# Masked cross-attention: the mask of the third key tile by a minimum over the exponentials

## The reference

```python
scores = jnp.einsum('bhqd,bhkd->bhqk', Q, K) * scale          # 16 x 16 x 100 x 361
scores = jnp.where(attn_mask[:, None, :, :], -jnp.inf, scores)
A = jax.nn.softmax(scores, axis=-1)
out = jnp.einsum('bhqk,bhkd->bhqd', A, V)
out = out.transpose(0, 2, 1, 3).reshape(Bv, Tq, Dm)
return jnp.einsum('btd,od->bto', out, Wo) + bo
```

## Time and profile before

| | before |
|---|---|
| median of three runs | 2042.7 us (2034.51 to 2044.05) |
| the profiled execution | 2037.27 us, its span 2035.6 us |
| masked cross-attention: first and last use of the mask on PE | 1520.3 and 1762.0 us |
| PE, DVE, ACT, POOL busy in the whole span | 76%, 47%, 26%, 25% |

### The profile page before, as it was taken

One profiled execution on the slowest core, in us unless ns is written; L12 is line 12 of the kernel. 1 busy time (PEld: TensorE's weight loads), 2 busy tenths in 40 slices (PEclk: granted clock), 3 DMA queues, 4 the chain that ended last, 5 costly groups with the idle time before them and its releaser, 6 DMA issues. The chain is left out here.

```text
span 2035.6 us, 33676 instructions
## 1 busy us (share of the span) xinstructions
PE 1553.0 (76%) x11689; PEld 1200.6 (59%) x11689; DVE 959.3 (47%) x2639; ACT 528.5 (26%) x1081; POOL 502.0 (25%) x448
## 2 busy tenths in 40 slices
PE   4898974799978846999999155677549999636992
PEld 2555642577755525888888132455227877535992
DVE  4446435677755621222222286566547777450111
ACT  1444231244432101211121011222114344211330
POOL 1112010322213552222221670100032332222003
PEclk9999996799988877999999577797769999857996
DMA  6754563766622205666665355543256565127994
GB/s 245 193 165 146 154 180 110 159 149 143 145 57 57 57 9 168 198 200 199 195 187 162 89 163 166 111 100 81 87 135 134 127 136 126 47 84 264 346 345 140
DMA packets 302577, 303.34 MB, mean 149 GB/s; under 512 B 130910, under 2 KB 273630, under 8 KB 296878
## 3 DMA queue, kind: packets, MB, share of 16 engines
q1 hardware_dynamic: 272142, 263.32, 46.3%
q0 software_dynamic: 19328, 28.35, 5.1%
q10 hardware_dynamic: 11040, 10.82, 1.6%
HBM read 217.29 MB, written 85.03 MB: 149 GB/s over the span
## 5 line engine op out<-in xcount | busy, mean ns | idle before, releaser
L1458 ACT ACTIVATE attn_prob<-attn_ps_prob 121x400 f32<-121x400 f32 (+2 forms) x448 | 221.7, 503 | 418.1 <-PE attn_ps_prob L1357 414.3
L1316 PE MATMUL attn_ps_score<-attn_k,attn_q 96*100 96x361 bf16 (+1 forms) x768 | 152.1, 304 | 69.3 <-DMA attn_k<-k_stack 59.7
L1357 PEld LDWEIGHTS attn_ps_prob<-attn_q,attn_k 128*121 128x121 bf16 (+2 forms) x1792 | 162.1, 137 | 36.5 <-issue 8.1
L2179 DVE TENSOR_TENSOR experts_up<-experts_act_,experts_ps_up 128x250 f32<-128x250 f32 x128 | 53.2, 415 | 266.7 <-ACT experts_act_ L2140 266.7
L1357 PE MATMUL attn_ps_prob<-attn_q,attn_k 128*121 128x100 bf16 (+2 forms) x1792 | 169.1, 219 | 4.5 <-DVE attn_q L1506 3.0
L1487 DVE TENSOR_REDUCE attn_nmax<-attn_ps_score 100x2 f32<-100x722 f32 (+1 forms) x160 | 145.7, 921 | 38.7 <-PE attn_ps_score L1316 37.3
L1479 DVE CUSTOM_DVE_ANT_0 attn_masked_score<-attn_ps_score,attn_mask 100x361 bf16<-100x361 f32 x256 | 124.6, 531 | 55.0 <-PE attn_ps_score L1316 44.3
L1590 POOL TENSOR_TENSOR attn_q<-attn_shift,consts_sb 32x800 bf16<-32x800 bf16 x64 | 97.1, 1518 | 187.1 <-DVE attn_shift L1512 187.1
L2068 POOL DMA_INDIRECT experts_xe<-ln_rows,experts_now x64 | 77.6, 1212 | 257.8 <-DVE experts_now L2171 232.7
L2097 PE MATMUL experts_ps_up<-experts_xt,experts_wg 128*128 128x250 f32 x512 | 130.7, 378 | 0.8 <-DVE experts_xt L2168 0.8
L2097 PE MATMUL experts_ps_up<-experts_xt,experts_wu 128*128 128x250 f32 x512 | 129.9, 376 | 0.0
(11 more groups left out here) (283 smaller groups left out, 2640.1 us busy)
## 6 DMA issues: line engine op xcount, KB each, us to landing
experts_w<-in_w SPq DMA_DIRECT2D x40, 1024.0 KB, 5.5
attn_k<-k_stack SPq DMA_DIRECT2D x64, 541.5 KB
k_stack<-mixer_part SPq DMA_DIRECT2D x32, 541.5 KB, 5.4
experts_wg<-in_wg SPq DMA_DIRECT2D x32, 512.0 KB
experts_wu<-in_wu SPq DMA_DIRECT2D x32, 512.0 KB
experts_wd<-in_wd SPq DMA_DIRECT2D x32, 512.0 KB, 5.2
attn_q<-q_stack SPq DMA_DIRECT2D x96, 150.0 KB
k_stack<-mixer_part SPq DMA_DIRECT2D x32, 361.0 KB, 6.0
```

The lines of the kernel that those rows point to most:

```text
L1316: ins = nc.tensor.matmul(out, q_sb[s][0:SHIFT_ROW, h // HH, h % HH, :], k_sb[s][0:SHIFT_ROW, h // HH, h % HH, :], start=True, stop=True)
L1357: ins = nc.tensor.matmul(out[0:rows_, j * T:(j + 1) * T], k_sb[s][:, h // HH, h % HH, at:at + rows_], q_sb[s][:, h // HH, h % HH, :], star ...
L1458: nc.scalar.activation(prob[0:rows_, q4 % 2, t, :], ps_prob[k % 2][0:rows_, 0:GT], ACT.Exp, scale=DH ** -0.5).then_inc(a_prob[s], 1)
```

## The change

The mask of the third key tile no longer enters the score bank by a matmul. The exponentials of this tile are taken of the unmasked scores, and VectorE then sets the masked ones to zero by a minimum (`weigh`, L1547 of the changed kernel) with a table `upper`, which holds 0 where a key is masked and 3e38 elsewhere. The table is made once per batch element: TensorE transposes the third tile of the mask into PSUM (`turn_mask`, L1370), VectorE compares and scales it (L1539). The first two tiles keep their mask matmul. `weigh_values` now waits for the minimum (`v_weight`) before its third tile. `WEIGH_AT` puts the minima of quarters 0, 1 and 2 at the start of slots 4, 7 and 10 of VectorE's order, that of quarter 3 at the start of the next step.

```diff
--- before.py
+++ after.py
@@ -1162,6 +1162,7 @@
 
     at_unit = {-(-(u + 1) * (NPU - (NKT > 1)) // NU) - 1: u for u in range(NU)}
     shift_by_vector = layer == 1
+    WEIGH_AT = {4: 0, 7: 1, 10: 2}
     if NKT > 1:
         LAST_AV, SHIFT_B, ROWS, TURN, OUT, SHIFT_A = 1, 2, 3, 5, 7, 9
         av_at = {3 * g + 4: g for g in range(NQ - 1)}
@@ -1193,6 +1194,7 @@
         ones_set = sem("ones_set")
         g_order = sem("g_order")
         v_apart = sem("v_apart")
+        pe_upper, v_upper, v_weight = pair("pe_upper"), pair("v_upper"), pair("v_weight")
 
         q_sb = [sbuf(f"q{s}", [P, 2, HH, T], BF16) for s in range(2)]
         k_sb = [sbuf(f"k{s}", [P, 2, HH, NK], BF16) for s in range(2)]
@@ -1213,6 +1215,7 @@
         if masked:
             mask8 = [sbuf(f"mask8_{s}", [T, NK], U8) for s in range(2)]
             mask = [sbuf(f"mask{s}", [T, NK], BF16) for s in range(2)]
+            upper = [sbuf(f"upper{s}", [P, T]) for s in range(2)]
             masked_score = sbuf("masked_score", [T, HH, NK], BF16)
         ps_score = psum("ps_score", [P, 4, 512])
         ps_prob = [psum(f"ps_prob{k}", [P, 512]) for k in range(2)]
@@ -1349,16 +1352,23 @@
                     elif n_prev is not None:
                         pe.wait_ge(a_prob[1 - s], n_prev * NPU + k - 1)
                     out = ps_prob[k % 2]
-                    if masked:
+                    by_matmul = masked and t < NKT - 1
+                    if by_matmul:
                         nc.tensor.matmul(out[0:rows_, 0:GT], mask[s][:, at:at + rows_], prog.c("tile_diag")[0:T, :],
                                          start=True, stop=False)
                     for j in range(G):
                         h = q4 * G + j
                         ins = nc.tensor.matmul(out[0:rows_, j * T:(j + 1) * T],
                                                k_sb[s][:, h // HH, h % HH, at:at + rows_],
-                                               q_sb[s][:, h // HH, h % HH, :], start=not masked,
-                                               stop=not masked or j == G - 1)
+                                               q_sb[s][:, h // HH, h % HH, :], start=not by_matmul,
+                                               stop=not by_matmul or j == G - 1)
                     ins.then_inc(pe_prob[s], 1)
+
+                def turn_mask(s, n):
+                    at, rows_ = KEYS[NKT - 1]
+                    pe.wait_ge(g_mask[s], n)
+                    nc.tensor.transpose(ps_misc[:].bitcast(BF16)[0:rows_, 0:T], mask[s][:, at:at + rows_],
+                                        ident_b[0:T, 0:T]).then_inc(pe_upper[s], 1)
 
                 def weigh_values(s, n, q4, n_prev):
                     if q4 == 0:
@@ -1366,7 +1376,10 @@
                         if n_prev is not None:
                             pe.wait_ge(a_acc[1 - s], n_prev)
                     for t, (_, rows_) in enumerate(KEYS):
-                        pe.wait_ge(a_prob[s], n * NPU + (q4 * NKT + t + 1 - NPU))
+                        if masked and t == NKT - 1:
+                            pe.wait_ge(v_weight[s], n * NQ + (q4 + 1 - NQ))
+                        else:
+                            pe.wait_ge(a_prob[s], n * NPU + (q4 * NKT + t + 1 - NPU))
                         for j in range(G):
                             ins = nc.tensor.matmul(ps_acc[32 * j:32 * j + 32, q4 * T:(q4 + 1) * T],
                                                    val[s][0:rows_, t, q4 * G + j, :],
@@ -1399,6 +1412,9 @@
                     for u in range(NU):
                         score_unit(s, n, u, n_cur)
                     shift_rows(s, n, 0)
+                    if masked:
+                        pe.wait_ge(v_shift[0][s], n)
+                        turn_mask(s, n)
                     values(s, n)
 
                 def step(s, n, n_prev, n_next):
@@ -1410,6 +1426,8 @@
                             weigh_values(s, n, av_at[k], n_prev)
                         if k == SHIFT_B:
                             pe.wait_ge(v_shift[0][s], n)
+                            if masked:
+                                pe.wait_ge(v_upper[s], n)
                             shift_rows(s, n, 1)
                         if n_prev is not None:
                             if k == ROWS:
@@ -1430,6 +1448,9 @@
                                     pe.wait_ge(v_shift[1][s], n)
                                 shift_rows(1 - s, n_next, 0)
                     if n_next is not None:
+                        if masked:
+                            pe.wait_ge(v_shift[0][1 - s], n_next)
+                            turn_mask(1 - s, n_next)
                         values(1 - s, n_next)
 
                 def tail(s, n):
@@ -1512,6 +1533,20 @@
                     nc.vector.tensor_copy(shift[h][SHIFT_ROW:P, :], ps_misc[:].bitcast(BF16)[SHIFT_ROW:P, 0:T]
                                           ).then_inc(v_shift[h][s], 1)
 
+                def turn_mask(s, n):
+                    rows_ = KEYS[NKT - 1][1]
+                    ve.wait_ge(pe_upper[s], n)
+                    nc.vector.tensor_scalar(upper[s][0:rows_], ps_misc[:].bitcast(BF16)[0:rows_, 0:T], 0.0, 3e38,
+                                            ALU.is_ge, ALU.mult).then_inc(v_upper[s], 1)
+
+                def weigh(s, n, q4):
+                    rows_ = KEYS[NKT - 1][1]
+                    ve.wait_ge(v_upper[s], n)
+                    ve.wait_ge(a_prob[s], n * NPU + ((q4 + 1) * NKT - NPU))
+                    here = prob[0:rows_, q4 % 2, NKT - 1, :].rearrange("p (g t) -> p g t", g=G)
+                    nc.vector.tensor_tensor(here, here, upper[s][0:rows_].unsqueeze(1).broadcast_to([rows_, G, T]),
+                                            ALU.min).then_inc(v_weight[s], 1)
+
                 def values(s, n):
                     for t, (_, rows_) in enumerate(KEYS):
                         ve.wait_ge(pe_val[s], n * NKT - (NKT - 1 - t))
@@ -1543,10 +1578,17 @@
                     for u in range(NU):
                         score_unit(s, n, u)
                     shift_rows(s, n, 0)
+                    if masked:
+                        turn_mask(s, n)
                     values(s, n)
 
                 def step(s, n, n_prev, n_next):
                     for k in range(NPU):
+                        if masked:
+                            if k == 0 and n_prev is not None:
+                                weigh(1 - s, n_prev, NQ - 1)
+                            if k in WEIGH_AT:
+                                weigh(s, n, WEIGH_AT[k])
                         if k == SHIFT_B:
                             shift_rows(s, n, 1)
                         if n_prev is not None:
@@ -1562,9 +1604,13 @@
                             if k == SHIFT_A:
                                 shift_rows(1 - s, n_next, 0)
                     if n_next is not None:
+                        if masked:
+                            turn_mask(1 - s, n_next)
                         values(1 - s, n_next)
 
                 def tail(s, n):
+                    if masked:
+                        weigh(s, n, NQ - 1)
                     to_rows(s, n)
                     turn(s, n)
                     project(s, n)
```

## The result

| | before | after |
|---|---|---|
| median of the runs | 2042.72 us (2034.51 to 2044.05, 4 runs) | 2123.89 us (2122.0 to 2125.4, 4 runs) |
| profiled execution, its span | 2037.27, 2035.6 | 2122.0, 2120.3 |
| mean granted clock | 0.875 | 0.861 |

A forecast was written before the change was run, and what follows sets the result against it. TensorE was taken to bound the masked stage. Its step was to grow from 15.56 to 19.9 us: +65 us over fifteen steps and 1.5 in the last, +67 on the 2042.7 median, giving 2110 us, range 2090 to 2142.

The forecast's parts named there:

- The walk: Masked cross-attention step followed in four legs between third-tile releases: period 19.9 us instead of 15.56, +4.36 us.
- guess of 0.08 us: Gap between a minimum's end and TensorE's start, guessed within 0 and 0.16; moves the sum by 5 us at most.
- near tie: Quarter 2 to quarter 3: TensorE's own work takes 3.81 us, just shorter than 3.93 us up to the minimum's release.
- hidden as said: VectorE's 16 tables, near 0.22 us each, cost nothing behind a 0.44 us wait for TensorE; uncovered, 3.5 us.
- The 10.9 us of removed matmuls: TensorE time freed by dropping the third tile's 64 mask matmuls at 0.17 us each, 0.68 us per step.
- Rival 1: Masked stage slows just as the walk says: 2110 us, own range 2098 to 2122; chance 0.60.
- rival 2: TensorE's clock falls in two to five masked-stage steps, adding 12 to 29 us: 2122 to 2139 us; chance 0.22.
- self-attention's busy share: Masked stage would fall to TensorE busy 15.0 of 19.9, the share of self-attention, which has a stretch at clock 0.59.
- Rival 3: GpSimd gets the ports first at quarter 2; a minimum waits up to 1.52 us, +23 us: 2133 us; chance 0.06.
- the lock: VectorE and GpSimd share SBUF ports exclusively; two-SBUF-input minima are concerned, but at quarter 2 it should cost nothing.
- Rival 4: Some stalls vanish as VectorE catches up; two of four legs at old length, +33: 2076 us; chance 0.07.
- Rival 5: TensorE finds the minima done; each step 0.53 us shorter, 8.5 us in all: 2034 us; chance 0.05.

The follow-up runs named there:

- e1_free: Changed kernel, but weighted sums do not wait for the minima, which read a tile of ones and write unread tiles; ratio 0.9988 to the kernel before.
- e6_late_sums: Changed kernel with TensorE's weighted sums moved to later slots, minima left where they stood; ratio 1.0008 to the kernel before.
- e7_both: Changed kernel with later weighted sums and earlier minima; ratio 0.9990 to the kernel before, steps 15.26 us.
- r_filler: Rerun of the changed kernel with useless matmuls filling TensorE's stalls at quarters 1 and 2; ratio 1.0354 to the kernel before, steps 19.46 us.
- e2_no_min: Changed kernel with the third key tile's mask left out altogether: no mask matmul, table, transpose or minimum; ratio 0.9962 to the kernel before.
- e4_mask_too: Changed kernel with the third tile's mask matmul kept beside the minimum; ratio 1.0411 to the kernel before, steps 20.68 us.
- r_changed: Changed kernel rerun unedited, on one chip beside the version with filled stalls; ratio 1.0403 to the kernel before, steps 20.42 us.
- e9_twice: Changed kernel with a second, unused minimum of the same size ahead of each of the 64; ratio 1.0826 to the kernel before.
- e10_twice_late: e7_both with a second, unused minimum ahead of each of the 64; ratio 1.0286 to the kernel before, steps 18.9 us.
- e3_early: Changed kernel with the minima of quarters 0, 1 and 2 moved earlier in VectorE's order; ratio 1.0068 to the kernel before, steps 16.35 us.

## Why the prediction held, step by step

**Order is the cause.** That is shown: the same 64 minima cost nothing when no one waits (e1_free) and nothing when the sums come later (e6_late_sums, e7_both), and 81 us where the change put them. The direction, the place and the mechanism were those of the forecast.

**The walk**, against the timeline of the kernel after:

| leg, release to release | predicted | measured |
|---|---|---|
| quarter 1 to quarter 2 | 5.00 | 1702.96 to 1707.91, 4.95 |
| quarter 2 by way of 3 to 0 | 4.97 + 4.65 = 9.62 | to 1717.37, 9.46 |
| quarter 0 to quarter 1 | 5.30 | to 1722.59, 5.22 |
| step | 19.92 | 19.63 |

This is one of the longer steps that keep the clock; they are 19.36 and 19.62 us by turns, 19.46 in the mean of r_filler, so the walk is 0.46 us a step too long. Its guess of 0.08 us between the end of a minimum and TensorE's start is 0.06 in the trace (1707.27 + 0.58 to 1707.91). Quarter 3 is the one difference in kind: its minimum ends at 1712.83, about when TensorE gets to its third tile by its own work. The prediction had this as a near tie (3.81 against 3.93). That makes 52 waits instead of 64.

**The terms.** The minimum was put at 0.57 us between 0.42 and 0.99, and the median is 0.571. The table measured 0.255 us, not 0.22, and is hidden as said. The 10.9 us of removed matmuls were mis-sized: e2_no_min gives some 5 us back when nothing waits. The walk did not use the 10.9: it had only the one missing at slot 8 and the one at slot 11, 0.17 us each, on its way, and e4_mask_too shows just these two, 0.17 us each. Why the 0.68 us per step of TensorE's time return only 0.34 is not settled; VectorE, which takes the scores in a fixed order, may set part of the old 15.60, but no run isolates that.

**The sum.** Predicted: +65 for fifteen steps, +1.5 for the last. Measured in thirteen steps, with the clock taken out: 13 x (19.46 - 15.60) = 50.2 us, so 3.86 us a step where the walk had 4.36. Over fifteen steps that is 58 us, 7 less than forecast. The remaining 10.65 us ahead of the first output and 3.29 in the last two steps are not free of the clock. A step and a half of the chain explains 6 of the 10.65, and one of the first minima takes 1.154 us beside GpSimd. But the changed kernel has a long stretch at 1.2 GHz there:

```profile
1532.00:1545.00 13.00, 12.43 (x89) 8.79 (x90) 7.36 (x29) 2.70 (x6) 2.96 (x2) 0.50 0.40 84
```

From its first mask matmul to its first output the kernel before has 1.00. How the other 4 us or so divide between this stretch and the rest was not measured. So it is partly luck that 50.2, 10.65 and 3.29 add up to 64 us, within 3 us of the forecast of 67: the walk was too high per step, and the clock at the start made up for it.

**The step that failed** is the choice between rivals 1 and 2. They are not alternatives: the chain came, and the clock fell on top of it. Rival 1 alone gave 2110 with an own range to 2122; measured were 2123.89, in the interval of rival 2 (2122 to 2139). The stated range reached further, by a dearer minimum (to 2135), which did not come, and by rival 2, which did, with the smaller chance. Its price of 12 to 29 us holds 12.5 and 16.6, but not as it was built: not two to five whole steps went cold at 5.9 us each. The thirteen steps of the change have nine separate stretches at 0.50 and so do those of r_changed, most of them only part of a step, at 1.4 to 1.8 us each; the longest steps in the run of the change are 23.24 and 21.3. Nor does the comparison with self-attention's busy share carry the forecast: TensorE's share, forecast as 75%, reads 164.34 of 200, 82%. A busy time counts the stretched matmuls and overlaps in full, so the total of the waits (62.1 us, forecast 70; longest 2.0, forecast near 2) is the better witness of standing still.

**Rival 3** did not come in 62 of 64 minima (the other two, 1.15 and 0.71 us, stood behind GpSimd in the first and in the last step): at quarter 2 the minimum gets there first (L1547 at 1707.27, before L1636 at 1707.39), as forecast, and GpSimd is the one held up. GpSimd in the kernel after, at quarter 2 and then at its other place:

```profile
1707.39 1.84 POOL L1636 TENSOR_TENSOR attn_q<-attn_shift,consts_sb 32x800 bf16<-32x800 bf16 x1 [1.58 <-DVE attn_shift L1533]
...
1715.33 1.52 POOL L1636 TENSOR_TENSOR attn_q<-attn_shift,consts_sb 32x800 bf16<-32x800 bf16 x1 [4.62 <-DVE attn_shift L1533]
```

The prediction took the lock from a cast, which has one operand and so says nothing of the rule for two; the minima bear that rule out. The margin is 0.12 us, and e9_twice and e10_twice_late show that the mechanism was real: with a further operation of this kind in the queue, it is a minimum that stands, for 1.32 us. **Rival 4** has no case: no leg came back to its old length but the one of quarter 3, in part. **Rival 5** needed VectorE about 2.07 us earlier than it is. e7_both in effect gives it that by the other end, and its steps are 0.34 us shorter than before, not the 0.53 of the rival.

## What to carry to other kernels

Between two engines that run fixed programs, an operation is priced by its place and not by its length: read when the consumer comes to it, and what the producer has queued ahead. Here 0.57 us at a late place cost 3.9 us per step, and the same operations cost nothing once the consumer's slot was moved one or two places down. So when work is moved to an engine with time to spare, move the consumer in the same edit; moving the operation up alone (e3_early) made the next thing in the queue late. And before that, ask what the saved work returns at best (here 5 us in 2043), by a version with nothing in its place.
